# A hand-written order for the last three head groups, and a two-pass ending of each tile with factors prepared on GpSimd, in a fused attention and FFN kernel

## What is computed

```python
def _L0_attn_ref(x, Wq, bq, Wk, bk, Wv, bv, Wo, bo, gamma, beta):
    ...                                   # Q, K, V, causal softmax(QK/sqrt(E)) V = ctx
    y = jax.nn.gelu(ctx @ Wo + bo, approximate=False)
    r = x + y
    mu = jnp.mean(r, axis=-1, keepdims=True)
    var = jnp.var(r, axis=-1, keepdims=True)
    return (r - mu) * jax.lax.rsqrt(var + 1e-05) * gamma + beta
...
x = L0_attn_x                             # (4, 512, 256)
xn = _layernorm(x, axis=-1)
s = _L0_attn_ref(xn, L0_attn_Wq, ...)
g = _silu(_L0_ffn_ref(xn, L0_ffn_w_gate_up, L0_ffn_w_down))
x = x + s * g
return x
```

## Time and profile before

| | us |
|---|---|
| median of 3 runs | 635.44 (635.09 to 635.5) |
| the profiled execution | 636.07 |
| its span, first to last instruction | 634.3 |
| TensorE busy | 604.5 (95%) |
| VectorE busy | 474.5 (75%) |
| ScalarE busy | 428.6 (68%) |
| GpSimd busy | 304.0 (48%) |

### The profile page before, as it was taken

The page is one execution under the profiler, slowest core; times in us unless marked ns, Lnnn a source line. Parts: engine busy times, 40 slices in busy tenths (PEclk is TensorE's granted clock), DMA queues, the critical chain, the costliest instruction groups (busy, mean ns, idle before and its releaser), DMA issues.

```text
span 634.3 us, 10638 instructions
## 1 busy us (share of the span) xinstructions
PE 604.5 (95%) x3342; PEld 522.7 (82%) x3342; DVE 474.5 (75%) x1122; ACT 428.6 (68%) x1023; POOL 304.0 (48%) x244
## 2 busy tenths in 40 slices
PE   8999999999799999999999999999999999999680
PEld 5888888888678889888888888898888989898560
DVE  6646565634888778888997887899878888987736
ACT  5433544526678787877978777797877769887550
POOL 1000000000165655645799555568965546897554
PEclk9999999999899999999999999999999999999896
DMA  8700222020577888866688897767799784879840
GB/s 261 249 2 33 67 100 66 11 65 34 166 200 236 215 243 248 224 200 166 206 218 240 248 232 214 207 169 198 242 271 244 196 243 137 230 222 280 222 108 34
DMA packets 68919, 113.28 MB, mean 179 GB/s; under 512 B 7553, under 2 KB 46593, under 8 KB 66817
## 3 DMA queue, kind: packets, MB, share of 16 engines
q1 hardware_dynamic: 68432, 112.30, 63.4%
q10 hardware_dynamic: 432, 0.33, 0.2%
HBM read 66.40 MB, written 46.20 MB: 178 GB/s over the span
## 4 chain that ended last, share of the span: by engine, by line
PE 80%; DMA 9%; DVE 4%; POOL 3%; ACT 2%; SPq 1%; issue 1%; ACTq 0%; POOLq 0%
PE bank L1027 31%; PE down_ps L1027 15%; PE down_ps L1177 12%; PE down_ps L1087 7%; PE bank L1056 7%; PE bank L1054 7%; DMA p_scratch<-probs 4%; DMA probs<-p_scratch 3%; PE bank L1138 2%; POOL pT_lo L570 2%; DVE probs L958 1%; DMA raw<-in_wd 1%; SPq L485 1%; ACT probs L704 0%; PE down_ps L1040 0%
## 5 line engine op out<-in xcount | busy, mean ns | idle before, releaser
L570 POOL TENSOR_TENSOR pT_lo<-probs,pT_hi 128x512 fp32r<-128x512 f32 x160 | 204.1, 1296 | 81.9 <-ACT pT_hi L714 81.2
L704 ACT ACTIVATE probs<-probs,least 128x512 f32<-128x512 f32 (+3 forms) x256 | 141.0, 554 | 39.0 <-DVE least L935 38.6
L935 DVE CUSTOM_DVE_ANT_0 probs<-bank,mask 128x512 f32<-128x512 f32 (+3 forms) x256 | 117.5, 485 | 28.7 <-PE bank L1027 26.4
L582 POOL TENSOR_TENSOR probs<-probs,inv 128x1024 f32<-128x1024 f32 (+1 forms) x32 | 46.9, 1468 | 144.1 <-DVE inv L944 144.1
L714 ACT ACTIVATE pT_hi<-probs 128x512 fp32r<-128x512 f32 x160 | 96.1, 625 | 16.7 <-DMA probs<-p_scratch 11.9
L958 DVE STREAM_TRANSPOSE probs<-probs 128x2048 f32<-128x2048 f32 (+1 forms) x64 | 95.4, 1491 | 0.3 <-POOL probs L582 0.3
L1177 PE MATMUL down_ps<-wo_lo,cT_hi 128*128 128x256 f32 x256 | 73.8, 288 | 6.1 <-DVE cT_lo L983 6.0
L1177 PE MATMUL down_ps<-wo_hi,cT_hi 128*128 128x256 f32 x256 | 72.1, 281 | 0.0
L1177 PE MATMUL down_ps<-wo_hi,cT_lo 128*128 128x256 f32 x256 | 72.0, 281 | 0.0
L1027 PE MATMUL bank<-kT_lo,qT_hi 128*128 128x384 f32 (+1 forms) x192 | 66.4, 346 | 3.7 <-DVE least L935 3.5
L1027 PE MATMUL down_ps<-pT_lo,v_hi 128*128 128x512 f32 x160 | 66.0, 412 | 2.5 <-POOL pT_lo L570 2.2
(11 more groups left out here) (146 smaller groups left out, 1403.7 us busy)
## 6 DMA issues: line engine op xcount, KB each, us to landing
p_scratch<-probs SPq DMA_DIRECT2D x16, 1024.0 KB, 4.4
probs<-p_scratch SPq DMA_DIRECT2D x64, 256.0 KB, 4.9
p_scratch<-probs SPq DMA_DIRECT2D x16, 768.0 KB, 5.8
probs<-p_scratch SPq DMA_DIRECT2D x64, 192.0 KB, 4.2
inv_b<-i_scratch SPq DMA_DIRECT2D x32, 256.0 KB, 5.2
p_scratch<-probs SPq DMA_DIRECT2D x16, 512.0 KB, 3.0
probs<-p_scratch SPq DMA_DIRECT2D x64, 128.0 KB, 4.8
p_scratch<-probs SPq DMA_DIRECT2D x16, 256.0 KB, 4.8
```

The source lines that it names most:

```text
L570: nc.gpsimd.tensor_tensor(lo[:].rearrange("p (a n) -> p a n", a=BLOCKS), turned(t, j), f32(hi[:]).rearrange("p (a n) -> p a n", a=BLOCKS), ...
L582: nc.gpsimd.tensor_tensor(p, p, factor, ALU.mult).then_inc(probs_made, 1)
L704: nc.scalar.activation(p, p, ACT.Exp, bias=least[:, u, g:g + 1], scale=-1.0, accum_out=total[:, n * T + t, g:g + 1]).then_inc(exp_done, 1)
L935: nc.vector.tensor_tensor_reduce(out=head_of(t, g), in0=ps[:, 0:(t + 1) * P].rearrange("p (k i) -> p k i", i=BLOCK), in1=mask_of(t), scale ...
```

## The change

Group numbers below are of the last three groups (13, 14, 15) and what runs beside them.

1. Each engine's list gets a tail, written out step by step, for all steps of groups 13 to 15 (with the P, c and O of group 12 that run beside them). `program()` puts it behind the periodic part. The same steps are issued, in another order.
2. Group 15 writes its probabilities into buffers of its own, `probs_last`, which lie where the weights of the projections were. Its masks wait for the last projection instead of for the low parts of group 14.
3. The steps of the last row's end become words of the tails: ty, tg, ts, tr, tp, to, td. ScalarE's tg for tile 3, which stood behind ch15.1, stands between ph15.1.0 and ph15.1.1.
4. GpSimd prepares gamma g and beta g + x for each tile (tp, three passes). VectorE then ends a tile by two passes: (r - mean) * gamma g right behind the statistics, and * rstd + (beta g + x) once the root is there. GpSimd's eight passes and VectorE's ten of before go.
5. LX of the last row (loads of `x_b`, `g_b`) stands ahead of the write of group 14's tile 1. The store of the third row stands ahead of the last two reads. The store of the last row of g stands behind the first IW, and LX waits for it.
6. GpSimd's last five out pieces of the third row stand together ahead of no14.1; nm of that row stands ahead of three low parts of group 14's Q.

```diff
+SCALAR_TAIL = """
+qh3-- e3.2-- ph2.0--- e3.0-- ph2.1--- e3.1-- e3.3-- ph2.2--- ch3--- ph1.0--- ph1.1--- ph0.0--- gelu- ch2---
...
+VECTOR_TAIL = """
...
+cl2- ri0 tt1 cl1- xn cl0- c3 tt0 cl3 ty3 c2 cl2 ts3 ty2 cl1 ts2 ty1 cl0 ts1 ty0 to3 ts0 to2 to1 to0
...
+def program(head, text, tail):
+
+    head, tail = [*listed(head, 0, 0)], [*listed(tail, LAST, B - 1)]
+    return head + [s for s in order(text) if s not in head and s not in tail] + tail
...
+    probs_last = [sb(f"probs_last{t}", [P, G * (t + 1) * P], F32, late) for t in range(T)]
+    gamma_g = sb("gamma_g", [P, T, D], F32, late)
+    beta_g = sb("beta_g", [P, T, D], F32, late)
...
+        def tile_factors(t):
+
+            i = TILE_READY["tp", t]
+            pool.wait_ge(proj_done, max(PROJECTED["Q", LAST, h] for h in range(G)))
+            pool.wait_ge(g_b_in, 16 * B)
+            pool.wait_ge(x_b_in, 16 * B)
+            nc.gpsimd.tensor_tensor(beta_g[:, t, :], g_b[:, t, :], beta_row, ALU.mult).then_inc(tile_chain_pool, 1)
+            nc.gpsimd.tensor_tensor(gamma_g[:, t, :], g_b[:, t, :], gamma_row, ALU.mult)
+            pool.wait_ge(tile_chain_pool, i)
+            nc.gpsimd.tensor_tensor(beta_g[:, t, :], beta_g[:, t, :], x_b[:, t, :], ALU.add).then_inc(tile_ready, 1)
...
-                if step == ("ch", PERIODS - 1, 1):
-                    tile_gelu_of(3)
-                elif step == ("ch", PERIODS - 1, 0):
-                    tile_gelu_of(2)
+                elif kind == "tg":
+                    tile_gelu_of(n)
...
+            r = res[:, t, :]
+            dve.wait_ge(tile_ready, TILE_READY["tp", t])
+            nc.vector.scalar_tensor_tensor(r, r, mv3[:, t, 0:1], gamma_g[:, t, :], ALU.subtract, ALU.mult).then_inc(tile_scaled, 1)
...
+            dve.wait_ge(tile_root, TILE_ROOT["tr", t])
+            dve.wait_ge(tile_scaled, TILE_VAR["ts", t])
+            nc.vector.scalar_tensor_tensor(r, r, rstd3[:, t:t + 1], beta_g[:, t, :], ALU.mult, ALU.add).then_inc(tile_out, 1)
...
-                    if n and t in BY_DRAM:
-                        dve.wait_ge(probsT_split, PT_SPLIT["pl", n - 1, t, t])
+                    if n == LAST:
+                        dve.wait_ge(proj_done, max(PROJECTED["Q", n, h] for h in range(G)))
+                    elif n and t in BY_DRAM:
+                        dve.wait_ge(probsT_split, max(PT_SPLIT["pl", n - 1, t, j] for j in range(t + 1)))
```

229 lines of the change are left out of this document (126 added, 103 removed).

## The result

The changed kernel takes 630.81 us (median of 4 runs, 630.68 to 632.16). The kernel before, run beside it, takes 635.27 us. The ratio is 0.9937, with a 95% interval of 0.9919 to 0.9954. That is faster, by 4.5 us (4.0 by the ratio) where 8.4 were forecast. The time lies in the stated range, but at its far end, 3.8 us above the forecast of 627.0.

The account below looks back on a forecast made before the run. TensorE was taken as full up to 592 us, then waiting for the probabilities in the drain and idle for the last 14.3 us. From 635.44 us, -7.1 and -1.3 gave 627.0; 8 in 10 range 623.5 to 631.5.

Parts of the forecast that it names:

- Part 1: Behind TensorE's last product: the rewritten ending takes 7.3 us in place of 14.4, -7.1 us, bounds -7.9 to -6.3.
- The 0.8 us for ts1 beside tp1 and tp0: VectorE's ending: two of ts1's passes are slowed beside GpSimd's, 0.4 to 0.5 us each, 0.8 us added.
- Part 2: The drain of group 15: the new order ends O15.0 1.3 us earlier, bounds -4.5 to +1.3.
- tt15.3 and W15.3 come 2 us earlier: Tile 3 of group 15: of 3.3 us from earlier scores, between 0.7 and all arrive; 2 us taken.
- W and R of tile 3 then have the same way: Group 15's probabilities: from the write's issue to the first low part stays 13.9 us.
- Rival A: The drain does not move, O15.0's end moves by 0 to +2 us; 629.3 us, chance 0.22.
- Now tile 2's data should be there, so the wait is gone: GpSimd's low parts of group 15: the 2.3 us wait goes; the list takes 16.1 us, 15.0 before.
- no waits of TensorE worth over 1.5 us before 585 us: Sign for the changed kernel's profile: TensorE has no waits worth over 1.5 us before 585 us.
- tg3 ahead of ph15.1.1 at nothing: ScalarE: the table load of 1.28 us lies beside O15.3 and costs nothing; without that cover, 1.3 us.
- B: Rival: the drain gives nearly all, tile 3's read lands over 3 us earlier; 623.6 us, chance 0.15.
- C: Rival: slower than before, as a late chain ahead of VectorE's m15.0.2 makes TensorE stand; 637 us, chance 0.05.
- D: Rival: in the ending, GpSimd's tp1 and tp0 come after VectorE wants them; 631.8 us, chance 0.05.

Follow-up runs that it names:

- e_drain: The kernel before with only the new written order of the last three groups, ending as before; 638.40 us, ratio 1.0037 to the kernel before.
- r_after: The changed kernel itself, unchanged, run and profiled a second time; 631.19 us, ratio 0.9923 to the kernel before.
- e_ending: The kernel before's order with only the new ending, at the places the ending had before; 630.89 us, ratio 0.9931 to the kernel before.
- e_tpcol: The changed kernel with GpSimd's factors for tiles 2, 1 and 0 cut to one column each; 629.44 us, ratio 0.9891 to the kernel before.
- e_end2: e_ending with the new ending moved to the changed kernel's places, old order kept; 629.91 us, ratio 0.9905 to the kernel before.
- e_q: The changed kernel with read R15.2 moved ahead of IR15.3 and W15.1 on SyncE; 632.53 us, ratio 0.9950 to the kernel before.
- e_both: The changed kernel with IR14.3 and IR14.2 ahead of W15.3, ph14.0.0 behind ph14.1.1 and pl14.0.0 behind no15.1; 631.81 us, ratio 0.9927 to the kernel before.
- e_st: e_end2 with O15.3 placed as in the changed kernel and the store of row 2 ahead of IR15.2 and R15.0; 628.14 us, ratio 0.9882.
- e_best2: e_end2 with O15.3 placed as in the changed kernel and read R15.2 ahead of W15.1 on SyncE; 633.06 us, ratio 0.9958 to the kernel before.

## Why the prediction was right in its first part and wrong in its second

**Part 1, behind the last product: 7.3 us instead of 14.4, -7.1.** The mechanism and nearly the size were right. In the trace 6.3 us are left (-8.1, just past the bounds -7.9 to -6.3), and on the new order the ending is worth 7.2 us (e_drain against r_after). The form of the sum was wrong, though: it begins at TensorE's last product, as if VectorE came to it free. In fact VectorE works with hardly a gap from ts3 on, and ts3, ts2 and the y of two tiles stand ahead of cl15.1 and cl15.0. By the timelines, TensorE's waits there were 0.79 and 1.60 us before, and are 1.49 and 1.47. The passes that I moved in front of the last product were costed at nothing. At the old places, on the old order, 8.5 us follow the last product, and the ending gives 2.2 us less than I had (e_ending: -4.9 in the traces). So it is partly luck that 7.2 came so near to 7.1: it took the statistics at their new places, whose price the sum did not hold.

The 0.8 us for ts1 beside tp1 and tp0 hit the kind: ts1's gamma pass takes 0.79 in after, one of 0.47 to 0.48 when free. All three held ones together lose 0.9, and 0.35 us of it reaches the end (e_tpcol). The Trainium skill, "SBUF — State Buffer", section "SBUF: two separate sides", has the loser of the lock blocked fully. Here the trace agrees at one place: VectorE's first pass of ts3 took 1.52 us, from 613.70 to 615.22, where 0.43 is free, beside GpSimd's pl15.0.0, 1.28 us from 613.65:

```profile
613.65 1.28 POOL L659 TENSOR_TENSOR pT_lo<-probs_last,pT_hi 128x512 fp32r<-128x512 f32 x1 [0.50 <-ACT pT_hi L801]
```

It ends 0.29 us behind the low part's end. That pass, not ts1's, was the dear one, and I had not costed it. At the gamma passes the trace differs: beside GpSimd passes of 0.73 us and more they lose 0.3 us, not a whole pass. The result that I worked out by the page, -6.4 for part 1, was not the better one.

**Part 2, the drain: -1.3. This is the step that failed.** In its place the last product came 1.6 us later in the trace of after (3.6 in r_after's, 2.0 in e_drain's), past the bound of +1.3, and the order cost 2.4 us of time under the old ending and, with less certainty, 1.1 to 2.0 under the new one (e_end2). With it came the sign of being wrong that I had named, a last product later than 620 us (622.61). The last low part was to end 0.9 us earlier and ended 2.2 us later. Of these 3.1 us, 0.5 is W15.3's issue, 0.6 the way of tile 3's data, and 2.0 GpSimd's list. Behind the last low part the chain to the last product went from 8.3 to 7.7 us, where I had 0.4 us of relief.

- "tt15.3 and W15.3 come 2 us earlier": about right, 1.5 us from the mark (the bare 582.35 against 582.76 hides it, since this execution was 1.1 us late at the mark). no14.1 was 4.0 us later from the mark, where I had 2.6; two more out pieces are 2.6 of it, and where the other 1.4 come from was not followed.
- "W and R of tile 3 then have the same way", 13.9 us: it was 14.5. R15.3 was issued 2.2 us earlier and landed 0.9 earlier: the read itself took 8.9 us and not 7.6, with both inverse broadcasts of group 14 and the read of its tile 0 now issued just ahead of it. Rival A had this, as an aside: the DMAs land as late as before.
- "Now tile 2's data should be there, so the wait is gone": this is the term that was furthest off, waits of GpSimd put at nothing. R15.2 was issued 0.3 us earlier than before and landed 1.4 us later, behind IR15.3 and W15.1 (e_q shows what taking these away gives the read; which of the two weighs more was not tried). GpSimd's list, forecast at 16.1 us, took 18.1, with 2.1 us of waits in it: 0.89 for tile 2's data, 0.49 for ph15.3.3, which itself waited 1.73 us for TensorE, and 0.25 and 0.50 for high parts that stand behind ch15.3 and ch15.2 on ScalarE. So tile 2's late landing is the largest single one and not the half of it.
- "no waits of TensorE worth over 1.5 us before 585 us": right by the letter, but TensorE has 0.6 us of idle time between +130 and +150 and 0.9 between +165 and +176, where before had none. The ql that I saw (put at 1.1 us, taken by slack) is 0.4 of it; whether slack took it, no run shows.
- tg3 ahead of ph15.1.1 at nothing: true in after, where the table load is done when y comes, and e_ending without this place began ts3 some 3 us later. It was not free everywhere: the gelu waited 0.80 us for y in r_after and 2.09 in e_end2, and ph15.1.1 and GpSimd behind it. By the Trainium skill, "ScalarE: Activation LUTs", section "What ACT_TABLE_LOAD costs", 1.38 us of drain belong to each load; the row again says no:

```profile
609.56 1.28 ACT L764 ACT_TABLE_LOAD   x1
610.85 0.42 ACT L764 ACTIVATE res<-res 128x256 f32<-128x256 f32 x1
```

**The rivals.** A (0.22, 629.3) was the nearest, and its first mechanism was there: IR14.3, behind W15.3, made VectorE wait 2.44 us. But it is not the cause. With both inverses early and R14.0 out of the way too (e_both), nothing is gained. Its second half, transfers that land as late as before, is what the traces bear out, for tile 3 and tile 2. B, C and D did not come. (D's time together with A should read 635.44 - 7.1 + 4.8 + 1 = 634.1, not 634.5.)

**What stays open.** Which of the two transfers ahead of R15.2 makes it late; what R15.2 further ahead gives when the store of row 2 is out of the way; what of TensorE's idle time at +165 to +176 the change could avoid; and how much of what the order costs is TensorE's clock, which no run here holds fixed. That the late landings cost the time is argued from the traces; no run put the bytes back in the order of before under the new order of the engines.

## What to carry to other kernels

A read that is issued earlier into a full queue need not land earlier (here 2.2 us of issue gave 0.9 us of landing, and 2.3 us gave nothing): sum the bytes in flight between issue and use, before giving an earlier issue any gain. And if an ending is rewritten, add up the work of the engine that does it from its first step on; counting from another engine's last product counts as free all that was moved ahead of it.

Look at what a table load or a first step waits for. Here the early steps moved forward together (tg3, O15.3, the store that y waits for) took e_ending's 0.9931 to e_st's 0.9882, 3.1 us, where the reordering of three head groups gained nothing. And when an experiment comes out slower than it should, see which wait ends last: in e_q and e_best2 it was a store that neither experiment was about.

## What the runs showed of the hardware

The time before the mark, where the kernels differ only in when the last row of g is stored, varied by 5.4 us between profiled executions (414.22 to 419.61), and by 2.7 us in the same kernel (after and r_after). Two traces can be compared only from a common event on.

TensorE's clock was granted differently in the same kernel: after had 1.00 in the whole drain, r_after 0.79 from 612 to 620 us. r_after's execution took 635.41 us, 4.7 more than after's: 2.7 of it before the mark, 2.0 behind it. In e_ending, after a wait of 3.62 us, the 12 products of an O came 0.21 us apart, 0.12 in the O before the wait, so at the lower of the two levels (1.2 GHz instead of 2.4):

```profile
595.60 0.58 PE L1242 MATMUL down_ps<-wo_lo,cT_hi 128*128 128x256 f32 x1 [3.62 <-DVE cT_lo L1057]
595.98 0.42 PE L1242 MATMUL down_ps<-wo_hi,cT_lo 128*128 128x256 f32 x1
596.19 0.41 PE L1242 MATMUL down_ps<-wo_hi,cT_hi 128*128 128x256 f32 x1
```

Such a stretch adds about 1.1 us to one O (12 x 0.09). With the time before the mark, it is one of two things seen here that make executions of one kernel differ.
